# Two attention and two mixture-of-experts layers on one core: unread products, keys, row stores and a table moved

## The chip, the core and the metric

One core of a Trainium2 chip runs the whole program. The core has a matrix engine (TensorE, PE in the rows), a vector engine (VectorE, DVE), a scalar engine (ScalarE, ACT), a general one (GpSimd, POOL) and a queue engine (SyncE, SP) that computes nothing and issues DMAs; ScalarE and GpSimd issue DMAs too. Each engine works through its own list of instructions in order, and they meet at semaphores: an instruction waits until a counter has reached a value. The metric is the time of the whole program on the device, in microseconds (us), median of several runs; less is better.

## What is computed

The input x holds 32 sequences of 64 tokens with 128 values, 2048 tokens in all; ctx has the same shape.

```python
x = x + xattn0(layernorm(x), ctx, ctx)      # 16 heads of 8, biases, softmax over the 64 keys
x = x + ffn0(layernorm(x))                  # 8 experts, 2 per token, silu(x Wg) * (x Wu), inner size 176
x = x + xattn1(layernorm(x), ctx, ctx)      # as the first, other weights
x = x + ffn1(x)                             # 8 experts, 2 per token, gelu(x W1 + b1) W2 + b2, inner size 512

def ffn1(x):
    logits = xf @ gate_w                    # the router
    topk_vals, topk_idx = top_k(logits, 2)
    topk_w = softmax(topk_vals)
    ...                                     # each chosen expert's output, weighed and summed
```

## The kernel before

**Stages.** The 2048 tokens are 16 tiles of 128 and 4 groups of 512. The stages follow each other: loads and projections of the context and the queries (0 to 31 us), the first attention, the first experts (dense: every expert on every token), the second attention, and the second experts, which are sparse. Products are made of float16 pairs (a high and a low half), which is why most things exist twice.

**Keys.** The projected keys lie in k_T. SyncE copies them to `keys`, in which the four heads of a block stand in separate columns, by DMAs of 8 rows each (`place_keys`, line 343): part 0 is the first group (tiles 0 to 3), part 1 the other three, 16 DMAs each. Scores of tile 4 and later wait for the 16 DMAs of part 1. Ahead of part 1 SyncE issues the three loads of the first experts' weights (lines 368, 369; `w_g`, `w_u`, `w_d` in the trace), five loads of constants (line 371: iota8, expert_rows, table, before16, filler_rows) and the first two chunks of the second experts' weights (line 374). Behind it come seventeen stores of filler rows to sorted_rows, which wait for the constants.

**The attention's pipeline.** `attention(l)` runs `step(t)` for t from -3 on each engine. In step t TensorE turns the probabilities of tile t+1 (line 1529), turns the maxima of tile t+2 (1579), makes the scores of tile t+3 in two halves (1681, 12 matmuls each) with the fold of tile t+2's maxima between them (1602), and weighs the values of tile t. VectorE takes the scores' maxima (`TENSOR_REDUCE`, line 1026), GpSimd splits them (758, 760), ScalarE copies and takes the exponentials. The opening is the steps -3 to 1, in which the pipeline fills.

**Unread products.** `unread_products(n, bank, c0, c1)` issues n matmuls of 512 columns whose result nothing reads. Before, they stand in the first routing, in the last steps of the second attention and ahead of the second experts, and none in the opening.

**Sorting rows.** In the second attention the tokens are sorted by expert. Tiles are taken in five parts (`SORT_PARTS`: tiles 0-3, 4-7, 8-9, 10-11, 12-15). VectorE chooses the experts of a part (`choose`) two steps behind its last tile and finds its row numbers (`locate`, which ends at line 1116) a step later. GpSimd then stores each tile's normalised rows twice, once for each of its experts, with an indirect DMA to sorted_rows: `scatter(t, c)`, line 783, numbered d = 2t + c, 32 in all. `STORED` says how many have been issued at the end of each step; the rest come behind the loop. The first 24 (tiles 0 to 11) are the early ones: SyncE loads the first five slots' tiles of 256 sorted rows (line 410) when these have landed, and the later ones when all 32 have. GpSimd also computes the reciprocal deviation of each tile (`rstd`, line 740), which VectorE's `row_shift` (966) and so ScalarE's normalisation wait for.

**Tables.** With the first parts' counts VectorE makes a table of the first five slots (`early_counts`, `early_tiles`, `early_rows`), and with all of them one of the other eighteen (`late_table`), both read by SyncE and TensorE. `shares` makes the two weights of each token.

**The second experts.** For each of the 23 slots TensorE turns the rows (1835), ScalarE and VectorE split them (`arrive`, 1349 to 1355), TensorE multiplies by W1 (`up`), ScalarE takes the gelu (633), VectorE splits the hidden values (1367, 1369), TensorE multiplies by W2 (`down`, two slots behind), and GpSimd stores the result.

## Time and profile before

| | us |
|---|---|
| timed runs, median of 3 | 430.56 |
| lowest and highest | 429.47, 435.54 |
| the profiled execution | 428.84 |
| its span in the trace | 427.0 |

| engine | busy us | share of the span |
|---|---|---|
| TensorE, matmuls | 365.1 | 85% |
| VectorE | 341.2 | 80% |
| ScalarE | 268.8 | 63% |
| GpSimd | 245.7 | 58% |

The profile is of one execution. A row of its timeline gives the start of an instruction or a merged run of them, its duration, engine, line, tiles and, in brackets, how long the engine was idle ahead of it and what ended that. A busy TensorE is not TensorE at its peak: its clock has two levels, and the column PEclk tells which was granted, 1.00 (2.4 GHz) or 0.50 (1.2 GHz); at the lower one the same matmuls take twice as long.

### The profile page before, as it was taken

What the parts mean: (1) busy time and instruction counts of PE and PEld (TensorE: products, weight loads), DVE (VectorE), ACT (ScalarE), POOL (GpSimd) and SP (SyncE); (2) the same over time, 40 slices, a digit from 0 to 9 for tenths busy, and PEclk for the clock granted to TensorE, in tenths of its full rate; (3) what the DMA queues carried; (4) which work ended last, traced back from release to release, by engine and by line L of the source; (5) the groups of instructions that cost most, each with busy time, mean ns of one, the idle gap of its engine ahead of it and who ended that gap; (6) DMA issues with size and microseconds to landing.
All of it is one profiled execution on the core that took longest, in us unless ns stands there. A gap on an engine that the chain in (4) does not pass through costs nothing.

```text
span 427.0 us, 12926 instructions
## 1 busy us (share of the span) xinstructions
PE 365.1 (85%) x4528; PEld 256.8 (60%) x4528; DVE 341.2 (80%) x978; ACT 268.8 (63%) x591; POOL 245.7 (58%) x362
## 2 busy tenths in 40 slices
PE   3977799998779999999998799898878899999900
PEld 2644566666446656666655567676634798888800
DVE  6876589998888787887876689988877899999707
ACT  3664588987457555666556788786722766767504
POOL 7860367777525558576661244456787356677630
PEclk9996899999999999999999999998996999999965
DMA  7358797000001111101002400001113223232136
GB/s 202 83 166 257 218 382 266 4 3 2 2 0 51 51 52 49 48 16 40 0 11 34 62 3 2 5 21 34 40 47 102 78 79 95 78 90 65 45 103 223
DMA packets 30837, 33.15 MB, mean 78 GB/s; under 512 B 3908, under 2 KB 22606, under 8 KB 30776
## 3 DMA queue, kind: packets, MB, share of 16 engines
q1 hardware_dynamic: 27164, 25.84, 21.2%
q0 software_dynamic: 2496, 5.18, 3.6%
q10 hardware_dynamic: 1116, 1.31, 1.0%
q8 instruction: 38, 0.62, 0.6%
q14 instruction: 23, 0.19, 0.1%
HBM read 15.22 MB, written 15.01 MB: 71 GB/s over the span
## 4 chain that ended last, share of the span: by engine, by line
PE 48%; DVE 17%; SPq 10%; issue 10%; POOL 9%; ACT 3%; DMA 2%; POOLq 0%; DVEq 0%; ACTq 0%
PE ps L1433 10%; PE ps L1435 9%; PE ps L1434 9%; SPq L353 5%; PE ps L1681 4%; PE ps L1529 3%; DVE area L1026 3%; POOL sorted_rows L783 3%; POOL area L819 2%; PE ps L1602 2%; PE ps L1815 1%; SPq L371 1%; POOL expert_sums L839 1%; PE ps L1835 1%; PE ps L1443 1%
## 5 line engine op out<-in xcount | busy, mean ns | idle before, releaser
L819 POOL TENSOR_TENSOR area<-area 128x512 f16<-128x512 f32 x44 | 51.0, 1159 | 41.8 <-ACT area L587 41.8
L839 POOL DMA_INDIRECT expert_sums<-area x46 | 49.7, 1081 | 27.1 <-ACT area L609 14.4
L1433 PE MATMUL ps<-w,area 128*128 128x128 f16 (+1 forms) x360 | 63.7, 219 | 0.3 <-POOL area L819 0.2
L1434 PE MATMUL ps<-w,area 128*128 128x128 f16 (+1 forms) x360 | 63.7, 219 | 0.0
L1435 PE MATMUL ps<-w,area 128*128 128x128 f16 (+1 forms) x360 | 63.7, 219 | 0.0
L1433 PE MATMUL ps<-area,w 128*128 128x512 f16 (+1 forms) x180 | 58.8, 327 | 3.1 <-DVE area L1349 1.4
L1434 PE MATMUL ps<-area,w 128*128 128x512 f16 (+1 forms) x180 | 58.5, 325 | 0.0
L1435 PE MATMUL ps<-area,w 128*128 128x512 f16 (+1 forms) x180 | 58.4, 325 | 0.0
L1026 DVE TENSOR_REDUCE area<-ps 128x8 f32<-128x512 f32 x64 | 41.2, 686 | 14.5 <-PE ps L1681 13.2
L583 ACT ACTIVATE area<-ps 128x512 f32<-128x512 f32 x44 | 26.1, 597 | 35.1 <-PE ps L1435 34.5
L633 ACT ACTIVATE area<-ps,b_now 128x256 f32<-128x256 f32 x92 | 36.2, 477 | 12.0 <-PE ps L1435 11.9
L1276 DVE SCALAR_TENSOR_TENSOR area<-ps,area 128x512 f32<-128x512 f32 x44 | 30.1, 683 | 14.3 <-ACT area L583 14.3
L1529 PE MATMUL ps<-ident,area 128*128 128x128 f32 x256 | 37.6, 291 | 2.5 <-ACT area L508 1.5
L1433 PEld LDWEIGHTS ps<-w,area 128*128 128x128 f16 x360 | 35.2, 98 | 6.2 <-POOL area L819 1.3
L1681 PE MATMUL ps<-keys,q_T 32*64 32x256 f16 x768 | 34.8, 283 | 4.6 <-DMA keys<-area 2.4
L1434 PEld LDWEIGHTS ps<-w,area 128*128 128x128 f16 x360 | 35.2, 98 | 4.8
L783 POOL DMA_INDIRECT sorted_rows<-w,area x32 | 31.8, 995 | 10.7 <-issue 9.9
L508 ACT ACTIVATE area<-ps 128x512 f32<-128x512 f32 x64 | 34.8, 599 | 2.3 <-PE ps L1602 1.6
L1435 PEld LDWEIGHTS ps<-w,area 128*128 128x128 f16 x360 | 35.2, 98 | 0.0
L1369 DVE TENSOR_TENSOR area<-area 128x512 f16<-128x512 f32 x46 | 32.1, 698 | 1.6
L1529 PEld LDWEIGHTS ps<-ident,area 128*128 128x128 f32 x256 | 29.4, 148 | 4.6 <-ACT area L508 3.9
L758 POOL CAST area<-area 128x16 bf16<-128x16 f32 x32 | 6.3, 198 | 44.9 <-DVE area L1026 33.9
(241 smaller groups left out, 1039.4 us busy)
## 6 DMA issues: line engine op xcount, KB each, us to landing
sorted_rows<-filler_rows SPq DMA_DIRECT2D x16, 528.0 KB, 6.3
w_stage<-in_L_ffn_W SPq DMA_DIRECT2D x8, 512.0 KB, 4.0
w<-sorted_rows SPq DMA_DIRECT2D x23, 132.0 KB
keys<-area SPq DMA_DIRECT2D x32, 48.0 KB
area<-in_ctx SPq DMA_DIRECT2D x4, 256.0 KB, 4.8
keys<-expert_sums SPq DMA_DIRECT2D x4, 256.0 KB, 5.4
keys<-expert_sums ACTq DMA_DIRECT2D x4, 256.0 KB, 6.2
out<-x_res SPq DMA_DIRECT2D x8, 128.0 KB, 1.9
```

Of the source, the lines that this page charges most:

```text
L508: nc.scalar.activation(probs[:, t % 2, h * HALF:(h + 1) * HALF], ps[:, 2 * (t % 2) + h, :], ACT.Exp, scale=float(HD) ** -0.5 / ASCALE ** 2 ...
L633: nc.scalar.activation(act_f[:, n % 4, f * ST:(f + 1) * ST], ps[:, n % 4, f * ST:(f + 1) * ST], ACT.Gelu, bias=b1_now[:, 2 * u + f, j:j + ...
L783: nc.gpsimd.indirect_dma_start(out=sorted_rows, out_offset=bass.IndirectOffsetOnAxis(ap=place[:, t, c:c + 1], axis=0), in_=rows32[:, t, :] ...
L819: nc.gpsimd.tensor_tensor(hid[:, n % 4, 1, :], gated[:, n % 4, :], hid[:, n % 4, 0, :], ALU.subtract).then_inc(q["lo"], 1)
L839: nc.gpsimd.indirect_dma_start(out=expert_sums, out_offset=bass.IndirectOffsetOnAxis(ap=to_row[:, j, h:h + 1], axis=0), in_=ys[j % OUTS][: ...
L1026: nc.vector.tensor_reduce(mx[:, v, h * hh:(h + 1) * hh], ps[:, 2 * v + h, :].rearrange("p (h k) -> p h k", k=SEQ), axis=AX.X, op=ALU.max). ...
L1369: nc.vector.tensor_tensor(hid1[:, n % 8, 1, :], act_f[:, n % 4, :], hid1[:, n % 8, 0, :], ALU.subtract).then_inc(q["lo"], 1)
L1433: pe.matmul(dst, lhs[0], rhs[0], start=start, stop=False, **kw)
L1434: pe.matmul(dst, lhs[0], rhs[1], start=False, stop=False, **kw)
L1435: return pe.matmul(dst, lhs[1], rhs[0], start=False, stop=stop, **kw)
L1529: mm = pe.matmul(ps[:, 4 + h, n * P:(n + 1) * P], probs[:, t % 2, c:c + P], ident[:, :], is_transpose=True, start=(n == 0), stop=(n == 3), ...
L1681: mm = pe.matmul(ps[64 * b:64 * b + 64, 2 * v + n // 2, HALF // 2 * odd:HALF // 2 * (odd + 1)].rearrange("p (j k) -> p j k", j=QUAD), q_T[ ...
```

## The change

Five edits, none of which changes what is computed.

```diff
-STORED = {8: 2, 9: 4, 10: 6, 11: 9, 12: 11, 13: 14, 14: 16, 15: 18, 16: 20}
+STORED = {7: 2, 8: 4, 9: 6, 10: 8, 11: 11, 12: 13, 13: 16, 14: 18, 15: 20, 16: 21}
...
@@ SyncE
             place_keys(0, 0)
             for c in range(3):
                 sp.dma_start(w_stage0[c].rearrange("p (a b) -> p a b", b=w_in[c].shape[2]), w_in[c]).then_inc(s["ch0_in"], 16)
+            place_keys(0, 1)
             for dst, name in ((iota8, "iota8"), (expert_rows, "expert_rows"), (table, "table"), (before16, "before16"), (filler_rows, "filler")):
...
             load_chunk(0)
             load_chunk(1)
 
-            place_keys(0, 1)
@@ VectorE, last_steps
                     residual(LAST + 1)
+                    statistics(LAST + 1)
                     row_shift(LAST)
                     early_tiles()
-                    statistics(LAST + 1)
                     row_shift(LAST + 1)
@@ VectorE, late_table is cut in two: its start, up to last_tiles(left), is now tiles_left()
-                late_table()
-                shares()
+                tiles_left()
                 arrive(0)
                 arrive(1)
+                late_table()
                 for j in range(MT):
...
                     if j + 2 < MT:
                         arrive(j + 2)
+                shares()
@@ TensorE, project_queries
+                if l == 0 and g >= 2:
+                    unread_products(2, 0, 0, 512)
                 pe.wait_ge(KV["xt"], n + 1)
@@ TensorE, attention, ahead of the steps
                     pe.wait_ge(s["zero"], 11)
+                    unread_products(4, 0, 0, 512)
                 pe.wait_ge(KV["q_lo"], GROUPS * (l + 1))
@@ TensorE, step(t), behind the turned probabilities
                     if l == 0 and t == -2:
                         output_bias()
+                        pe.wait_ge(KV["v_lo"], 2 * GROUPS)
+                        unread_products(6, 5, 0, 512)
+                    if l == 0 and t == 0:
+                        unread_products(3, 6, 0, 512)
@@ TensorE, step(t), behind the second half of the scores
                         scores(t + 3, (t + 3) % 2, 1).then_inc(q["s_ps"], 1)
+                    if l == 0 and t == -2:
+                        unread_products(2, 5, 0, 512)
+                    if l == 0 and t == -1:
+                        pe.wait_ge(s["bo"], 2)
+                        unread_products(2, 6, 0, 512)
@@ TensorE, last_steps
-                        unread_products((1, 9, 1)[j - LAST + 1], 5, 0, 512)
+                        unread_products((1, 4, 1)[j - LAST + 1], 5, 0, 512)
                         row_logits(j)
-                    unread_products(5, 5, 0, 512)
+                    unread_products(8, 5, 0, 512)
                     part_ranks(4)
@@ TensorE, experts1
                 first_biases(0)
-                unread_products(7, 5, 0, 512)
+                unread_products(3, 5, 0, 512)
                 turn(0)
                 turn(1)
-                unread_products(4, 6, 0, 512)
+                unread_products(3, 6, 0, 512)
```

SyncE's list around the second placement of the keys (the 16 DMAs of 8x2x1536), ahead of the filler stores, first as it was:

```order
L369 DMA w<-in_L_ffn_w_d 128x11x128
L371 DMA iota<-in_iota 128x8
L371 DMA expert_rows<-in_expert_rows 128x1408
L371 DMA table<-in_table 128x192
L371 DMA before<-in_before 128x128
L371 DMA filler_rows<-in_filler 128x528
L374 DMA w_stage<-in_L_ffn_W 128x2x512 x2
L353 DMA keys<-area 8x2x1536 x16
L384 DMA sorted_rows<-filler_rows 256x1x528 x16
```

And the same place in the changed kernel:

```order
L369 DMA w<-in_L_ffn_w_d 128x11x128
L353 DMA keys<-area 8x2x1536 x16
L372 DMA iota<-in_iota 128x8
L372 DMA expert_rows<-in_expert_rows 128x1408
L372 DMA table<-in_table 128x192
L372 DMA before<-in_before 128x128
L372 DMA filler_rows<-in_filler 128x528
L375 DMA w_stage<-in_L_ffn_W 128x2x512 x2
L384 DMA sorted_rows<-filler_rows 256x1x528 x16
```

Seven loads that stood ahead of the keys stand behind them; the three weight loads stay ahead.

TensorE's list in the first attention's steps -2 and -1 (transpose of the maxima, scores and fold, turned probabilities), before the change:

```order
L1579 MATMUL ps<-identb,area 128x128
L1681 MATMUL ps<-keys,q_T 64x256 x12
L1602 MATMUL ps<-minus_ones,area 128x512 x2
L1681 MATMUL ps<-keys,q_T 64x256 x12
L1529 MATMUL ps<-ident,area 128x128 x8
```

And with it; line 1447 is the unread product:

```order
L1447 MATMUL ps<-ctx_T,wT 128x512 x6
L1590 MATMUL ps<-identb,area 128x128
L1697 MATMUL ps<-keys,q_T 64x256 x12
L1613 MATMUL ps<-minus_ones,area 128x512 x2
L1697 MATMUL ps<-keys,q_T 64x256 x12
L1447 MATMUL ps<-ctx_T,wT 128x512 x2
L1536 MATMUL ps<-ident,area 128x128 x8
```

Six products stand ahead of the first transpose and two between the scores and the turned probabilities.

VectorE's list at the start of the second experts: 1151 and 1153 end the part of the table that is now `tiles_left`, 1159 to 1178 are its second part, 1349 to 1355 an arrival of slots. Before:

```order
L1153 TENSOR_REDUCE area<-area 128x8
L1159 TENSOR_TENSOR expert_rows<-table,area 128x144
L1161 TENSOR_REDUCE area<-expert_rows 128x18
L1163 TENSOR_SCALAR area<-area 128x18
L1168 TENSOR_TENSOR expert_rows<-expert_rows,area 128x144
L1170 TENSOR_REDUCE area<-expert_rows 128x18
L1172 SCALAR_TENSOR_TENSOR area<-area,table 128x18
L1174 SCALAR_TENSOR_TENSOR area<-area 128x18
L1176 TENSOR_SCALAR area<-area 128x18
L1178 TENSOR_SCALAR area<-area,table 128x18
L1130 TENSOR_SCALAR area<-area 128x16
```

And the same place now, where 1352 to 1358 are the arrivals:

```order
L1153 TENSOR_REDUCE area<-area 128x8
L1352 TENSOR_TENSOR area<-ps,area 128x256
L1354 TENSOR_SCALAR area<-w,area 128x2
L1356 TENSOR_TENSOR area<-area,w 128x2
L1358 TENSOR_TENSOR area<-area,table 128x2
L1352 TENSOR_TENSOR area<-ps,area 128x256
L1354 TENSOR_SCALAR area<-w,area 128x2
L1356 TENSOR_TENSOR area<-area,w 128x2
L1358 TENSOR_TENSOR area<-area,table 128x2
L1159 TENSOR_TENSOR expert_rows<-table,area 128x144
```

The nine instructions of the second part stand behind the two arrivals and directly ahead of the first hidden tile; the shares (1130 and two more) have gone to the end.

## Rows read from the trace of the kernel before

**Rows 1.** Page, chain that ended last: shares of the span by engine
```profile
PE 48%; DVE 17%; SPq 10%; issue 10%; POOL 9%; ACT 3%; DMA 2%; POOLq 0%; DVEq 0%; ACTq 0%
```

**Rows 2.** Chain in order of time, 0 to 60 us: start, duration, what
```profile
26.69 1.22 SPq L369
...
27.95 4.40 SPq L371
...
35.28 0.71 SPq L353
...
46.26 2.92 DMA keys<-area
```

**Rows 3.** Timeline of TensorE, 29 to 63 us: start, duration, line, tiles, idle ahead
```profile
31.57 1.13 PE L1681 MATMUL ps<-keys,q_T 32*64 32x256 f16 x24 [1.33 <-DVE q_T L941]
...
34.75 0.29 PE L1579 MATMUL ps<-identb,area 128*128 128x128 bf16 x1 [1.60 <-POOL area L760]
...
49.22 0.53 PE L1681 MATMUL ps<-keys,q_T 32*64 32x256 f16 x12 [2.37 <-DMA keys<-area]
...
54.03 0.63 PE L1681 MATMUL ps<-keys,q_T 32*64 32x256 f16 x12
...
58.09 0.53 PE L1681 MATMUL ps<-keys,q_T 32*64 32x256 f16 x12
```

**Rows 4.** Windows: length, busy time (instructions) by engine, granted clock, DMA share, GB/s
```profile
34.00:40.00 6.00, 5.18 (x48) 3.03 (x48) 2.69 (x8) 2.50 (x6) 0.84 (x4) 0.50 0.94 302
51.00:54.00 3.00, 3.00 (x36) 2.67 (x35) 2.79 (x8) 1.92 (x4) 1.72 (x3) 0.50 1.05 388
324.00:330.00 6.00, 6.00 (x20) 3.25 (x20) 4.81 (x23) 2.49 (x6) 4.76 (x5) 0.50 0.46 137
333.00:338.00 5.00, 3.59 (x45) 3.10 (x43) 4.83 (x13) 3.90 (x12) 0.77 (x1) 1.00 0.20 57
338.00:402.00 64.00, 63.33 (x812) 57.00 (x810) 60.73 (x162) 44.15 (x119) 43.03 (x40) 1.00 0.27 77
```

**Rows 5.** DMA issues, 0 to 60 us: size of each, us from issue to landing
```profile
w<-in_L_ffn_w_d SPq DMA_DIRECT2D x1, 704.0 KB, 9.3
```

**Rows 6.** Timeline of TensorE, 307 to 345 us
```profile
324.83 3.17 PE L1443 MATMUL ps<-ctx_T,wT 128*128 128x512 f16 x7
...
335.20 0.28 PE L1433 MATMUL ps<-area,w 128*128 128x256 f16 x1 [1.41 <-DVE area L1349]
```

**Rows 7.** Timeline of VectorE, 24 to 56 us: reduces of tiles 1 and 2
```profile
37.22 1.29 DVE L1026 TENSOR_REDUCE area<-ps 128x8 f32<-128x512 f32 x2 [3.17 <-PE ps L1681]
...
41.27 1.29 DVE L1026 TENSOR_REDUCE area<-ps 128x8 f32<-128x512 f32 x2 [0.20 <-PE ps L1681]
```

**Rows 8.** Timeline of VectorE, 262 to 345 us
```profile
295.50 0.22 DVE L1116 TENSOR_REDUCE area<-area 128x8 uint32<-128x64 f32 x1
...
318.12 0.16 DVE L966 SCALAR_TENSOR_TENSOR shift<-mv_now,rstd 128x1 f32<-128x1 f32 x1 [1.07 <-POOL rstd L740]
...
325.44 0.31 DVE L1159 TENSOR_TENSOR expert_rows<-table,area 128x144 f32<-128x144 f32 x1
...
327.45 0.23 DVE L1178 TENSOR_SCALAR area<-area,table 128x18 f32<-128x18 f32 x1
...
328.88 0.42 DVE L1349 TENSOR_TENSOR area<-ps,area 128x256 f16<-128x256 f32 x1 [0.62 <-ACT area L603]
...
332.35 0.43 DVE L1367 CAST area<-area 128x512 f16<-128x512 f32 x1 [1.66 <-ACT area L633]
```

**Rows 9.** Timeline of GpSimd, 262 to 350 us
```profile
295.29 1.10 POOL L783 DMA_INDIRECT sorted_rows<-w,area  x1 [0.50 <-issue]
...
316.54 0.96 POOL L783 DMA_INDIRECT sorted_rows<-w,area  x1 [0.30 <-issue]
317.52 0.57 POOL L740 TENSOR_TENSOR rstd<-mean_var,minus_half 128x1 f32<-128x1 f32 x1
```

**Rows 10.** Timeline of SyncE, 323 to 325 us: first load of sorted rows
```profile
324.64 0.40 SPq L410 DMA_DIRECT2D w<-sorted_rows  x1
```

3 lines of the change are left out of this document (2 added, 1 removed).

## Prediction, made before the changed kernel ran

> **What bounds the kernel now.** The page's chain [rows 1] gives half of the span to TensorE and 10% to SyncE's queue, an engine that computes nothing: a queue is on the path, and the chain in order of time says where. From 27.95 to 46.9 us it is SyncE issuing DMAs, ending with the second placement of the keys [rows 2]. The TensorE rows show the other end of it: the scores of tile 4 wait 2.37 us for those keys, so TensorE stood there ready at 49.22 - 2.37 = 46.85 [rows 3]. The windows then say at which clock TensorE got there: the granted clock was 0.50 (1.2 GHz) from 34 to 40 us and again from 51 to 54 us, and it is full (2.4 GHz) in the long expert stage, where TensorE is busy 63.33 of 64 us [rows 4]. So three things bound the stretches that the change touches: keys and a halved clock in the first attention's opening, GpSimd's stores and VectorE's table work between the second attention and the experts, and TensorE itself from about 338 us to the end of the products. Work saved ahead of the expert stage moves everything behind it; TensorE time lost inside that stage is lost.
>
> **Keys ahead of the constants.** Between the load of w_d and the first key issue SyncE spends 35.28 - 27.95 = 7.33 us on seven loads. The first of them takes 4.40 us, though its data is 4 KB: it is not its own size that holds it but the 2.1 MB of expert weights queued just ahead, 704 KB each, the last issued at 26.69 and landing 9.3 us later [rows 2, 5]. An undisturbed issue here takes 0.43 (bound from the other side: 0.71, a key issue), so some 3.97 us of the 4.40 is a hold-up that will now fall on the first key issue. The placement therefore starts 7.33 - 3.97 = 3.4 us sooner. The issues themselves (from 35.28 to 46.26, at 0.73 us each) and the landing of 2.92 us behind the last stay. The keys land at 46.26 + 2.92 - 3.4 = 45.8. If the hold-up did not fall on the keys at all it would be 41.8; if it lasted until the weights have landed (26.69 + 9.3 = 36.0) it would be 49.9. I take 45.8, because the hold-up ended at 32.35 whatever came behind it. The seven loads and the filler stores behind them go out later, the loads by sixteen issues or 12 us. Their readers are the routing behind this attention, the first experts and the second attention's sort; between lie more than ten steps of 4.06 us [rows 3], which cover them. Without that cover it would be up to 12 us. SyncE also waits for VectorE's low halves of the last keys; the chain goes from issue to issue at 27.95 with no wait for VectorE in it, and if it were late, each 0.1 us would count.
>
> **Unread products in the opening.** One product costs 3.17/7 = 0.45 us at half clock [rows 6], so about 0.23 at full. Two lie ahead of each of the last two query projections, where TensorE waits for ScalarE's copy anyway; four ahead of the first scores (wait 1.33, of which GpSimd's clearing of weights takes a part); six ahead of the first transpose of maxima, where it waits 1.60 [rows 3]: 6 x 0.23 = 1.4. All hidden, at full clock. The remaining 2 + 2 + 3 lie between dependent pieces; they cost 1.6 us of TensorE, in gaps that full clock opens. 
> What that is worth is set by the engine that is next in line. The reduce of tile 1 on VectorE starts at 37.22 after 3.17 us idle [rows 7]. In front of it stand the transpose, two halves of scores and the fold, 37.22 - 34.75 = 2.5 us at half clock [rows 3] and, with ScalarE's copy of 0.3 in it that doesn't shrink, about 1.5 at full: it starts about 0.95 sooner. From there VectorE has work up to the reduce of tile 2 at 41.27, ahead of which it is idle only 0.20, and that gap goes too: 1.15, say 1.2 us sooner, and that difference is carried on. TensorE comes to tile 4 at 46.85 - 1.2 = 45.65. Keys at 45.8 and chain at 45.65 meet; either alone would have been worth little. Tile 4's scores start at 45.8 instead of 49.22: **-3.4 us**. With the wait of 2.37 gone the half-clock stretch behind it goes too: the next scores came 54.03 - 49.22 = 4.81 us later, and the undisturbed step behind that is 58.09 - 54.03 = 4.06 [rows 3]: **-0.8 us**. The opening: -4.2.
>
> **Stores a step sooner, statistics ahead.** GpSimd is two stores ahead from the seventh step on and one ahead at the end of the loop. The store's two prices are the wait for its row numbers and what it delays. At the eleventh step the first store now belongs to tile 4, whose row numbers VectorE finishes at 295.50 + 0.22 = 295.72 [rows 8]; the store stood at 295.29 [rows 9] and moves to about 296.2. That is 0.9 us on GpSimd with the deviations of tile 10 and the maxima of tile 15 queued behind it. The deviation is read at the end of VectorE's step and the maxima only behind TensorE's next transpose, so most of it is covered: I book +0.3, and +0.1 for the same at the seventh step: **+0.4** (bounds 0, all covered, and 0.9 + 0.9, none).
>
> At the end the deviation of tile 15 runs at 317.52, behind two stores (the second at 316.54; 0.96 and an idle 0.30 each, 1.27 from one to the next); VectorE's shift waits 1.07 us for it [rows 8, 9]. With its statistics taken ahead of tile 14's shift and the six table instructions behind that, some 1.6 us sooner, they are no longer late, and with one store in that place the deviation runs at 317.52 - 1.27 = 316.25. Tile 15's normalisation, its logits, the choice and the row numbers all follow 1.27 us sooner. The last early store is the fourth behind this deviation and now the third: 2 x 1.27 = 2.5 us sooner. The first load of sorted rows, issued at 324.64 [rows 10], is issued at 322.1 and lands near 324.3 (2.2 us, an estimate below the keys' 2.92 of rows 2, since this load is spread over 128 partitions).
>
> **Products and table ahead of the experts.** TensorE runs seven and four products around the first two tile transposes, at half clock (324 to 330 us [rows 4]), and VectorE works through the second table meanwhile. Now three and three. The seven start at 324.83, so now at 323.55; three take 1.35 at half clock; the transposes run from about 324.9 (the load is there), and VectorE's arrivals start at 325.9 where they started at 328.88. They take 1.8, and now the table's second part stands behind them, 325.44 to 327.68 or 2.24 us: VectorE is free for the first hidden tile at 325.9 + 1.8 + 2.2 = 329.9, against 332.35 [rows 8]: -2.4. If the eight products ahead of the last ranks hold the clock at full, everything on TensorE there halves and it is 329.1: -3.25. I take the middle, **-2.8**.
>
> That move has a price, because the table now lies between the arrivals and the first hidden tile. The products of tile 0 and 1 no longer wait, but those of tile 2 need VectorE's third arrival, behind the hidden parts of tile 0. TensorE waited 1.41 us there [rows 6]. Now VectorE reaches the first hidden tile 1.8 + 2.24 = 4.06 us after its arrivals start, where it was 332.35 - 328.88 = 3.5 [rows 8], and TensorE, with one product fewer ahead of tile 0 and those at full clock if it holds, starts that tile about 0.9 sooner after the arrivals. The wait grows by 0.6 + 0.9 to 2.9 us (bounds 1.4 + 0.6 = 2.0, and 1.4 + 2.24 = 3.6). A wait of 1.41 left the clock at 1.00 (333 to 338 [rows 4]); one of 2.37 was followed by half clock over all of 51 to 54. I take 3.4 us of it (those three and the parts around them that stretch TensorE's step to 4.81), in a stage where TensorE has 1% to spare: half of that is lost, **+1.7**.
>
> The shares, three small instructions, go into VectorE's wait for the sums at the end, which lasts through the last products, stores and loads: nothing.
>
> **The sum.** -3.4 - 0.8 + 0.4 - 2.8 + 1.7 = -4.9. The profiled execution took 428.84 us (span 427.0 and 1.8 around it): 423.9. The three timed runs have a median of 430.56, 1.7 above the profiled one; -4.9 from there is 425.7. I predict 425.0, between the two, which is -4.9 from 429.9; the rivals are counted from there.
>
> **Rivals.** (A) The clock holds through the 2.9 us wait: -6.6, 423.3. For it: 1.41 did no harm. Against: 2.37 did. Chance 0.17. The Trainium skill (TensorE: Matmul & The Clock Gate, section Why this matters for your kernels) advises against idle gaps of over about 3 us; by it a gap of 2.9 would just pass and this rival would be the result. The trace disagrees at 2.37.
> (B) The products don't keep the clock. Then the four behind the scores cost 0.45 each and the three others a part: TensorE comes to tile 4 at about 48.9, the keys are long there, and the opening gives 0.3 + 0.8 = 1.1 instead of 4.2: -1.8, 428.1. For it: GpSimd's clearing and VectorE's queries leave gaps that can't be filled. Chance 0.12.
> (C) The expert stage gives back more than the late part gained: the half clock lasts twice as long, as it did for all of 324 to 330 [rows 4], and costs 3.4 instead of 1.7: -3.2, 426.7. For it: a wait of 2.9 is longer than any other in these rows. Against: TensorE is busy without a gap behind it. Chance 0.16.
> (D) Slower. SyncE is held until the weights have landed, at 36.0, later than the 35.28 at which the placement starts now. Keys at 49.9, 0.7 later; TensorE, early by 1.2, waits 4.3 us and pays two half-clock stretches, 3.4 instead of the 0.8 of now: +0.7 + 2.6 - 0.7 (the rest of the sum) = +2.6, 432.5. It decides against the change once the keys land later than the 49.2 of now and the wait for them has grown enough to cost a second stretch; up to 49.2 the rest of the sum keeps the sign. Against it: the hold-up in the trace ends at 32.35. Chance 0.05.
>
> **Chances and range.** The forecast has 0.50. Around it 421.5 to 429.5 holds A, B, C and a microsecond of scatter either way; D and larger upsides are outside. Two per cent, 8.6 us, is about what a measurement of this kernel can tell from no change; only A with keys and chain both at their better bounds comes near it: faster 0.08, same 0.90, slower 0.02.
>
> **What would show it.** Keys: the first key issue starts at 27.95 and takes some 4.7, the last packet lands at 45 to 46; tile 4's scores wait under 0.5. Clock: 1.00 in 34 to 47; if 0.50, B. Steps behind it 4.06 apart. Deviation of tile 15 directly behind one store; first load of sorted rows 2.5 us sooner than the rest of the shift. TensorE's wait before tile 2's products: 2.9, and the clock 0.50 within 4 us of it. Wrong would be the prediction if the two halves of the opening don't meet, or if the stores' waits at steps seven and eleven are passed on in full.

## The result, and the profile after

The changed kernel takes 426.14 us (median of 20 executions, 424.07 to 431.17) beside 429.44 for the kernel before (20 executions, 427.27 to 435.54; its first three, known at the time of the prediction, had 430.56). The ratio is 0.9935, with a 95% interval of 0.9907 to 0.9963: between 1.6 and 4.0 us saved, 2.8 by the ratio, where 4.9 were forecast. (Executions over 1.5% above the fastest of their kernel are left out of the ratios but not of the medians, so the two do not divide exactly.) The profiled execution of the changed kernel, 430.2 us with a span of 428.4, is one of its longer ones, and longer than that of the kernel before (427.0). What made it longer is the main finding below.

The opening went as forecast. The timeline of TensorE of the changed kernel, 29 to 56 us (start, duration, line, tiles, idle ahead):

```profile
31.91 1.14 PE L1697 MATMUL ps<-keys,q_T 32*64 32x256 f16 x24
33.44 1.47 PE L1447 MATMUL ps<-ctx_T,wT 128*128 128x512 f16 x6
35.10 0.23 PE L1590 MATMUL ps<-identb,area 128*128 128x128 bf16 x1 [0.20 <-POOL area L760]
...
45.99 0.53 PE L1697 MATMUL ps<-keys,q_T 32*64 32x256 f16 x12
...
49.98 0.30 PE L1697 MATMUL ps<-keys,q_T 32*64 32x256 f16 x3
```

L1697 is the scores, L1447 the unread products. Where [rows 3] have waits of 1.33 and 1.60 us there are none and 0.20; the scores of tile 4 start at 45.99 with no wait for the keys (before: 49.22, after a wait of 2.37), those of tile 5 at 49.98 (54.03), those of tile 6 at 54.05 (58.09). Behind the first scores (31.91, before 31.57) tile 4 stands 14.08 us, where it stood 17.65. SyncE's share of the chain fell from the 10% of [rows 1] to 1%:

```profile
PE 51%; DVE 15%; POOL 13%; issue 11%; DMA 4%; ACT 3%; SPq 1%; POOLq 0%; ACTq 0%; DVEq 0%
```

SyncE's timeline has the sixteen key issues in one row; the kernel before first, then the changed one, in which they stand ahead of the constants:

```profile
35.28 11.66 SPq L353 DMA_DIRECT2D keys<-area  x16
```

```profile
28.04 12.94 SPq L353 DMA_DIRECT2D keys<-area  x16
```

The windows of the changed kernel (length, busy time and instructions of PE, PEld, DVE, ACT and POOL, granted clock, DMA share, GB/s):

```profile
34.00:40.00 6.00, 5.25 (x70) 2.73 (x68) 3.61 (x9) 3.15 (x7) 0.83 (x4) 1.00 0.52 89
236.00:246.00 10.00, 10.00 (x100) 6.47 (x101) 4.55 (x9) 6.18 (x13) 2.25 (x7) 0.51 0.21 30
274.00:284.00 10.00, 10.00 (x106) 7.90 (x104) 6.26 (x22) 5.37 (x13) 4.67 (x9) 0.50 0.04 14
305.00:311.00 6.00, 6.00 (x72) 4.90 (x71) 3.48 (x16) 3.75 (x9) 3.94 (x5) 0.50 0.13 41
328.00:332.00 4.00, 3.51 (x14) 1.99 (x15) 2.35 (x13) 1.15 (x5) 3.08 (x4) 0.57 0.47 154
333.00:338.00 5.00, 3.49 (x37) 3.01 (x35) 4.76 (x15) 3.89 (x12) 3.00 (x3) 1.00 0.19 61
```

The opening (34 to 40) is at full clock, where [rows 4] had 0.50. But three rows of the second attention, in which the change moves only GpSimd's stores, stand at half clock (1.2 GHz). Before, all three stretches were at 1.00 (305 to 311 too); here are the first two:

```profile
236.00:246.00 10.00, 7.69 (x138) 4.75 (x133) 6.19 (x11) 8.57 (x17) 2.37 (x7) 1.00 0.40 58
274.00:284.00 10.00, 10.00 (x174) 7.49 (x173) 9.22 (x32) 8.79 (x23) 3.82 (x8) 1.00 0.03 9
```

So the profiled execution was four microseconds ahead at 230 us and four behind at 318 us. The second attention's first scores and the residual of tile 15, before (L1681 and the first L992 row) and after (L1697 and the second):

```profile
234.29 1.14 PE L1681 MATMUL ps<-keys,q_T 32*64 32x256 f16 x24 [0.78 <-DVE q_T L941]
...
314.26 0.28 DVE L992 SCALAR_TENSOR_TENSOR x_res<-ps,x_res 128x128 f32<-128x128 f32 x1
```

```profile
230.19 1.14 PE L1697 MATMUL ps<-keys,q_T 32*64 32x256 f16 x24 [0.77 <-DVE q_T L941]
...
318.25 0.28 DVE L992 SCALAR_TENSOR_TENSOR x_res<-ps,x_res 128x128 f32<-128x128 f32 x1
```

From one to the other the kernel before needed 79.97 us and the changed one 88.06. That is where the traced gain went. The 20 times of the changed kernel differ with their mean clocks, which do not say where in the program the clock was at half: eleven lie between 424.07 and 426.32 at a mean clock of 0.959 to 0.972, one at 426.93 and 0.960, eight between 427.61 and 431.17 at 0.939 to 0.955.

The late part, VectorE's timeline (the shift and the first hidden tile) and TensorE's wait ahead of slot tile 2, in the changed kernel:

```profile
320.85 0.16 DVE L966 SCALAR_TENSOR_TENSOR shift<-mv_now,rstd 128x1 f32<-128x1 f32 x1 [0.22 <-POOL rstd L740]
...
329.50 0.42 DVE L1352 TENSOR_TENSOR area<-ps,area 128x256 f16<-128x256 f32 x1 [1.44 <-ACT area L603]
...
333.24 0.23 DVE L1178 TENSOR_SCALAR area<-area,table 128x18 f32<-128x18 f32 x1
333.38 0.42 DVE L1370 CAST area<-area 128x512 f16<-128x512 f32 x1
```

```profile
336.06 0.28 PE L1437 MATMUL ps<-area,w 128*128 128x256 f16 x1 [1.51 <-DVE area L1352]
```

The first hidden tile stands 15.13 us behind the residual of tile 15 (333.38 - 318.25), where it stood 18.09 behind it (332.35 in [rows 8], less 314.26). The shift's wait of 1.07 is 0.22. The wait ahead of slot tile 2 is 1.51, not the forecast 2.9, and 333 to 338 is at full clock. The half clock that there is stands ahead of it, at 328 to 332.

### The profile page after: what moved, and what is told of

It is laid out like the page before. It is cut to its first block, busy times and chain, and to the rows that moved or that the text cites. A ratio compares the mean times of both kernels' runs of the same rounds, so it can differ in the third digit from the quotient of the medians.

```text
span 428.4 us, 12955 instructions
## 1 busy us (share of the span) xinstructions
PE 372.4 (87%) x4542; PEld 261.3 (61%) x4542; DVE 341.1 (80%) x978; ACT 269.7 (63%) x591; POOL 242.1 (57%) x362
## 3 DMA queue, kind: packets, MB, share of 16 engines
HBM read 15.22 MB, written 15.01 MB: 71 GB/s over the span
## 4 chain that ended last, share of the span: by engine, by line
PE 51%; DVE 15%; POOL 13%; issue 11%; DMA 4%; ACT 3%; SPq 1%; POOLq 0%; ACTq 0%; DVEq 0%
PE ps L1437 9%; PE ps L1439 8%; PE ps L1438 8%; PE ps L1697 6%; POOL sorted_rows L783 5%; PE ps L1536 4%; DVE area L1026 4%; POOL expert_sums L839 3%; PE ps L1489 2%; PE ps L1509 2%; PE ps L1613 2%; POOL area L819 2%; DMA keys<-expert_sums 2%; PE ps L1831 1%; PE ps L1547 1%
## 5 line engine op out<-in xcount | busy, mean ns | idle before, releaser
L839 POOL DMA_INDIRECT expert_sums<-area x46 | 46.3, 1007 | 29.0 <-ACT area L609 18.7
L1536 PE MATMUL ps<-ident,area 128*128 128x128 f32 x256 | 39.5, 302 | 1.3 <-ACT area L508 1.0
L1697 PE MATMUL ps<-keys,q_T 32*64 32x256 f16 x768 | 35.7, 289 | 0.9 <-DVE q_T L941 0.8
L1536 PEld LDWEIGHTS ps<-ident,area 128*128 128x128 f32 x256 | 31.3, 155 | 3.3 <-ACT area L508 2.4
L758 POOL CAST area<-area 128x16 bf16<-128x16 f32 x32 | 6.3, 198 | 45.8 <-DVE area L1026 34.8
```

Of the source, the lines that this page charges most:

```text
L839: nc.gpsimd.indirect_dma_start(out=expert_sums, out_offset=bass.IndirectOffsetOnAxis(ap=to_row[:, j, h:h + 1], axis=0), in_=ys[j % OUTS][: ...
L1536: mm = pe.matmul(ps[:, 4 + h, n * P:(n + 1) * P], probs[:, t % 2, c:c + P], ident[:, :], is_transpose=True, start=(n == 0), stop=(n == 3), ...
L1697: mm = pe.matmul(ps[64 * b:64 * b + 64, 2 * v + n // 2, HALF // 2 * odd:HALF // 2 * (odd + 1)].rearrange("p (j k) -> p j k", j=QUAD), q_T[ ...
```

## Experiments

Since the clock moves everything behind it, the runs are read in four pieces that do not mix: from the first scores of attention one to those of attention two (opening and what follows), from there to tile 15's residual (second attention), from there to the first hidden tile, and from the residual to the end of the span. All runs in one table, us; "half" is the sum of the stretches at half clock inside the piece, to about a microsecond:

| kernel | median | ratio to before, 95% | to attention two | half | second attention | half | residual to hidden | residual to end |
|---|---|---|---|---|---|---|---|---|
| before | 429.44 | | 202.72 | 10 | 79.97 | 3 | 18.09 | 112.74 |
| changed | 426.14 | 0.9935 (0.9907 to 0.9963) | 198.28 | 0 | 88.06 | 27 | 15.13 | 110.15 |
| e1_keys | 429.04 | 0.9987 (0.9957 to 1.0017) | 201.19 | 14 | 82.63 | 10 | 16.73 | 111.63 |
| e2_products | 428.97 | 0.9977 (0.9950 to 1.0004) | 200.80 | 3 | 80.82 | 3 | 16.88 | 111.73 |
| e3_opening | 427.44 | 0.9940 (0.9905 to 0.9975) | 198.31 | 0 | 80.77 | 3 | 18.12 | 112.65 |
| e4_late | 428.89 | 0.9978 (0.9951 to 1.0005) | 201.10 | 14 | 80.64 | 3 | 15.12 | 110.27 |
| e5_stores | 428.37 | 0.9978 (0.9948 to 1.0007) | 198.29 | 0 | 83.50 | 14 | 18.62 | 113.25 |
| e6_fill | 426.25 | 0.9926 (0.9900 to 0.9953) | 198.31 | 0 | 85.20 | 10 | 15.22 | 110.65 |
| e7_table | 427.62 | 0.9934 (0.9893 to 0.9975) | 198.29 | 0 | 87.74 | 27 | 14.75 | 109.99 |
| e8_seven | 429.33 | 0.9947 (0.9899 to 0.9995) | 198.29 | 0 | 88.10 | 27 | 15.71 | 110.18 |
| e9_open2 | 425.39 | 0.9909 (0.9883 to 0.9935) | 198.29 | 0 | 83.79 | 14 | 15.43 | 111.31 |
| e10_all_gaps | 423.25 | 0.9859 (0.9833 to 0.9885) | 198.31 | 0 | 79.73 | 0 | 15.83 | 110.62 |
| e11_changed | 428.82 | 0.9962 (0.9929 to 0.9994) | 198.28 | 0 | 87.67 | 27 | 15.12 | 109.93 |
| e12_before_filled | 427.84 | 0.9955 (0.9925 to 0.9984) | 201.21 | 14 | 79.43 | 0 | 18.06 | 112.77 |

The medians of the kernel before, run beside each group, were 430.18 (e1 to e4), 429.23 (e5 to e8), 430.19 (e9 to e11) and 429.74 (e12). Pieces come from one traced execution each. Groups ran at different times, so kernels of different groups are compared by their ratios.

### The opening: each half alone, and both

e1 moves the keys alone:

```
             for c in range(3):
                 sp.dma_start(w_stage0[c]...).then_inc(s["ch0_in"], 16)
+            place_keys(0, 1)
             for dst, name in ((iota8, "iota8"), ...
...
-            place_keys(0, 1)
             sp.wait_ge(s["init"], 16 * 5)
```

> The kernel before with one edit: the second placement of the keys is issued ahead of the five small loads and the first chunk. My account of the opening: the keys land near 45.8 us (they did at 49.18), TensorE's chain is untouched and comes to tile 4 at 46.85, the clock is still 0.50 in 34 to 40 us. Tile 4's scores start at 46.85 with no wait (49.22 after 2.37 before), the half clock behind that wait goes, tile 6's scores start at 54.9 instead of 58.09: -3.2 us in the whole, 0.9925 of the kernel before. Rival, that the two edits of the opening have to come together: the keys alone bring under 1 us (tile 6 at 57 or later). Rival, that the first key issue is held until the weights have landed: keys at 49.9, tile 4 no sooner than before, +0.5.

e2 adds the products alone:

```
+                if l == 0 and g >= 2:
+                    unread_products(2, 0, 0, 512)
...
+                    unread_products(4, 0, 0, 512)
                 pe.wait_ge(KV["q_lo"], GROUPS * (l + 1))
...
+                        pe.wait_ge(KV["v_lo"], 2 * GROUPS)
+                        unread_products(6, 5, 0, 512)
+                    if l == 0 and t == 0:
+                        unread_products(3, 6, 0, 512)
...
+                    if l == 0 and t == -2:
+                        unread_products(2, 5, 0, 512)
+                    if l == 0 and t == -1:
+                        pe.wait_ge(s["bo"], 2)
+                        unread_products(2, 6, 0, 512)
```

> The kernel before with one edit: the unread products in the first attention's opening; the keys stay where they were. My account: the clock is 1.00 in 34 to 47 us, TensorE comes to tile 4 about 1.2 us sooner (45.65) and waits 3.6 us instead of 2.37 for keys that land at 49.2 as before; tile 4's scores start at 49.2; the longer wait is followed by half clock as the shorter one was. In the whole 0 to +0.5 us. Rival, that the products do not hold the clock: 0.50 remains in 34 to 40 us, TensorE arrives at 48.9 and waits 0.3; again no more than 0.8 saved. Rival, that a shorter stretch of half clock is worth its length anyway: -1.2.

e3 is both, and nothing of the rest.

> The kernel before with both edits of the opening and nothing else. My account: tile 4's scores at 45.8 to 46.0 with a wait under 0.5, tile 6's at 54.0, -4.2 us against the kernel before, one microsecond more than the keys alone. The late part is as before: the first hidden tile is computed as long behind tile 15's residual as before (18.1 us). Rival (the later edits carry the gain, the second attention gives the opening's gain back): under 2 us.

TensorE's timeline of e1: the keys are issued by 41.5 and are there, and still tile 4's scores (the last row) start at 48.96.

```profile
35.63 0.23 PE L1579 MATMUL ps<-identb,area 128*128 128x128 bf16 x1 [1.60 <-POOL area L760]
...
41.86 2.12 PE L1529 MATMUL ps<-ident,area 128*128 128x128 f32 x8
...
48.96 0.86 PE L1681 MATMUL ps<-keys,q_T 32*64 32x256 f16 x12
```

Its windows show why: the clock did not come back at 41 us, as it had in the trace of the kernel before.

```profile
34.00:40.00 6.00, 4.33 (x45) 2.75 (x48) 3.23 (x7) 2.12 (x5) 0.83 (x4) 0.70 0.51 89
40.00:49.00 9.00, 9.00 (x98) 5.50 (x92) 5.87 (x14) 5.72 (x12) 2.73 (x6) 0.50 0.68 181
```

e4 and e12 have the opening of the kernel before unchanged, and their executions did the same: half clock for 14 us in one piece, 201.1 and 201.2 us to the second attention. Tile 4's scores in e4's timeline have no wait for the keys, though the keys come as late as before:

```profile
49.12 0.53 PE L1685 MATMUL ps<-keys,q_T 32*64 32x256 f16 x12
```

Against those, e1's 201.19 is no gain at all. My -3.2 for the keys alone was wrong (by the times -0.6, between -1.8 and +0.7): it took the 46.85 of one execution for the time at which TensorE arrives, and that hung on when the clock came back. Why it comes back at 41 us in one execution and at 49 in others is not shown. In e2's trace TensorE is as expected: TensorE arrives 14.14 us behind its first scores (33.05; 15.28 before, so 1.14 sooner, forecast 1.2), waits for the keys, and half clock follows the wait (49 to 53). The scores of tile 4 in its timeline:

```profile
48.79 0.53 PE L1693 MATMUL ps<-keys,q_T 32*64 32x256 f16 x12 [1.60 <-DMA keys<-area]
```

To the second attention e2 needs 200.80, 0.3 less than e4. By the times it gains 1.0 us (-2.1 to +0.2), which does not tell my 0 to +0.5 from the rival's -1.2.

Together, e3 needs 198.31 us, 2.8 less than e4 and e12 and 4.4 less than the trace of the kernel before. All nine traces with the complete opening give 198.28 to 198.31, at full clock. The two edits do have to meet; measured, the pair is worth 2.6 us by the ratio of e3 (1.1 to 4.1), where I expected 4.2. The products both close gaps and add to TensorE's busy time, and no run tells which of the two holds the clock.

### The late edits alone, the stores, the table, the seven products

e4 is the changed kernel with the edits of e1 and e2 taken out again.

> The changed kernel with the two edits of the opening undone, so only the stores a step sooner, the statistics of tile 15 ahead, the split table and the moved products remain. The opening is as before (tile 4's scores at 49.22). From tile 15's residual to the first hidden tile 15.1 us, where the kernel before has 18.1 and the changed one 15.1; wait ahead of slot tile 2's products 1.4 to 1.6 with the clock at 1.00. In the whole -2.4 to -2.8 us (0.994). If opening and late part add up, the changed kernel should be 6.6 us faster than before; it was measured 3.3 faster, so a rival is that something between them costs 3 us: then this kernel alone shows under 1 us of gain.

The piece from the residual to the first hidden tile is 15.12, the same as in the changed kernel and 3.0 below 18.1. To the end of the span the gain is 2.5 against the kernel before. But e1 and e2, which have none of the late edits, end at 111.6 and 111.7; ahead of the experts their clock was at half for 3 us, and for 7 in before, e3 and e12, which end at 112.7 to 112.8. e4 has 3 as well, and against e1 and e2 the late edits are worth 1.4. The median says 0.9 us (ratio, -2.1 to +0.2), below what I expected. The rival's number, under 1 us, came true, but not its reason that something between costs 3, since the second attention took 80.64. Opening and late part, 2.6 and 0.9 by their ratios, make 3.5, and the changed kernel 2.8: they add up within the intervals.

e5 puts the stores back:

```
-STORED = {7: 2, 8: 4, 9: 6, 10: 8, 11: 11, 12: 13, 13: 16, 14: 18, 15: 20, 16: 21}
+STORED = {8: 2, 9: 4, 10: 6, 11: 9, 12: 11, 13: 14, 14: 16, 15: 18, 16: 20}
```

> The changed kernel with one part undone: the stores are placed one step later again, as in the kernel before. Theory (the stores cost what I booked): GpSimd's waits of 0.64 and 0.74 us at the eleventh step and of 1.88 at the seventh go, about 0.4 us sooner at the residual of tile 15; the last early store and the first load of sorted rows come 1.27 us later and the deviation of tile 15 is back behind two stores, with the table's first part to hide it. From the residual of tile 15 to the end 111.4 us (112.74 before, 110.15 in the changed kernel). In the whole +0.5 to +1.0 us against the changed kernel. Rival (the waits at the stores hand their delay on to TensorE and are what costs the second attention its time): from the second attention's first scores to the residual of tile 15 it takes 2 us less than in the changed kernel in the median, and this kernel is the faster one by 1 us or more.

GpSimd's timeline of e5, and below it VectorE's shift of tile 15:

```profile
315.08 1.03 POOL L783 DMA_INDIRECT sorted_rows<-w,area  x1 [0.20 <-issue]
316.42 0.96 POOL L783 DMA_INDIRECT sorted_rows<-w,area  x1 [0.30 <-issue]
317.40 0.57 POOL L740 TENSOR_TENSOR rstd<-mean_var,minus_half 128x1 f32<-128x1 f32 x1
```

```profile
318.00 0.16 DVE L966 SCALAR_TENSOR_TENSOR shift<-mv_now,rstd 128x1 f32<-128x1 f32 x1 [1.47 <-POOL rstd L740]
```

The deviation of tile 15 starts 3.25 us behind its residual (314.15), as in the kernel before (317.52 - 314.26 = 3.26), though the statistics are ahead here. In the changed kernel it is 2.00 (320.25 - 318.25). So the statistics' new place alone brings nothing while two stores stand in front. The stores alone would not have brought the 1.26 us either. In VectorE's timeline of the kernel before the last of tile 15's statistics is

```profile
316.90 0.15 DVE L962 TENSOR_SCALAR mean_var<-mv_now 128x1 f32<-128x1 f32 x1
```

and ends at 317.05, 2.79 behind the residual, where the deviation started at 3.26: with one store fewer and the statistics late it could have started some 0.5 sooner (an estimate from this row; no run has the stores alone). This is a second pair that has to meet. The first load of sorted rows is 10.34 behind the residual (324.49), before 10.38, changed 7.84 (326.09): the 2.5 us hang on the stores, and by the same estimate in part on the statistics. The end cannot be compared, since e5's trace has half clock over nearly all of 318 to 333:

```profile
318.00:333.00 15.00, 14.10 (x65) 8.77 (x66) 9.50 (x57) 4.86 (x13) 9.64 (x10) 0.54 0.31 90
```

On the price of the earlier stores: from the wait at step eleven to the residual, e5 takes 22.05 us and e3, with the stores late too, 22.06; e4, with them early, 22.2. From the first scores to that wait e4 takes 58.4, e2 and e3 58.7 to 58.8, so nothing is lost there. The stores' waits cost at most 0.1 to 0.2 us, not the 2 that the rival wanted and less than the 0.4 I booked. GpSimd's wait for row numbers is there (0.64 us at 297.99 in the changed kernel), but it is covered.

e7 computes the second table in one piece again, e8 puts seven and four products back:

```
                 tiles_left()
+                late_table()
                 arrive(0)
                 arrive(1)
-                late_table()
```

```
-                unread_products(3, 5, 0, 512)
+                unread_products(7, 5, 0, 512)
                 turn(0)
                 turn(1)
-                unread_products(3, 6, 0, 512)
+                unread_products(4, 6, 0, 512)
```

> The changed kernel with the second table's experts and rows computed in one piece, ahead of the arrivals, as before. In the trace of the changed kernel VectorE is idle 1.44 us ahead of the arrivals and the table's second part takes 2.14 behind them; in one piece the arrivals start 0.8 later and the first hidden tile is no longer held by the table but by ScalarE. Theory: the split is worth next to nothing, the first hidden tile stands 15.1 +-0.4 us behind tile 15's residual as with the split. Rival (the split is what brought the hidden tile forward): 17 or more, +2 us in the whole.

> The changed kernel with seven and four unread products around the first two tile transposes ahead of the experts, instead of three and three. Theory: the loads of the sorted rows land while the seven run, so the transposes start some 1.1 us later (4 x 0.27, as the three took 0.82 in the trace of the changed kernel), the first hidden tile by 1.1 to 1.4 us, from tile 15's residual to the end 111.3. Rival (the extra products hold the clock at full where it fell at 328, and pay for themselves): 0 to -0.5 us.

With the table in one piece the first hidden tile is 14.75 us behind the residual and the end 109.99; with it split 15.13 and 110.15. The split is worth nothing or less. With seven and four products the hidden tile is 0.58 later and the end the same (110.18): less than the 1.1 to 1.4 I expected, and nothing by the end. So what is left of the late part is mainly the stores with the statistics; the moved products of the last steps and the shares were not tried alone.

### Where the second attention's clock goes

e11 is the changed kernel once more.

> The changed kernel once more, beside the two with filled gaps: 426.1 median, as before. If the place of the half clock differs from execution to execution, its trace shows a second attention of other length than the 88.06 us of the first trace, 80.8 at the shortest.

The median was 428.82 and not the 426.1 expected, 2.7 us above the median of the first 20 executions of the same kernel. Its trace has 87.67 us in the second attention, with falls at 235, 276 and 303. Of the twelve times five are 425.81 to 427.59 at a clock of 0.951 to 0.960, seven 428.00 to 430.37 at 0.939 to 0.950. So what varies with the time is how long the clock is at half; the ratio this time was 0.9962, and 0.9935 the first time, within each other's intervals. In the timeline of TensorE of e11, these gaps stand ahead of the falls, the first three within 7 us; behind the one at 294 the clock did not fall here, but in the kernel before it fell behind the same gap (293 to 296):

```profile
230.20 1.14 PE L1697 MATMUL ps<-keys,q_T 32*64 32x256 f16 x24 [0.77 <-DVE q_T L941]
233.38 0.23 PE L1590 MATMUL ps<-identb,area 128*128 128x128 bf16 x1 [0.58 <-POOL area L760]
235.88 1.97 PE L1536 MATMUL ps<-ident,area 128*128 128x128 f32 x8 [1.04 <-ACT area L508]
274.71 0.33 PE L1718 MATMUL ps<-ident,w 128*128 128x128 f32 x1 [1.68 <-DVE area L978]
294.02 0.33 PE L1718 MATMUL ps<-ident,w 128*128 128x128 f32 x1 [1.38 <-DVE area L978]
303.84 0.27 PE L1590 MATMUL ps<-identb,area 128*128 128x128 bf16 x1 [1.79 <-issue]
```

The test is to fill them. e6 was the first try:

```
+                else:
+                    unread_products(3, 0, 0, 512)
                 pe.wait_ge(KV["q_lo"], GROUPS * (l + 1))
...
+                    if l == 1 and t == -2:
+                        unread_products(2, 2, 0, 512)
+                    if l == 1 and t == TILES - 3:
+                        unread_products(6, 0, 0, 512)
...
+                        if l == 1:
+                            unread_products({6: 5, 10: 5, 12: 3}.get(t, 0), 2 * v, 0, 512)
                         scores(t + 3, v, 0).then_inc(q["s_half"], 1)
...
+                    if l == 1 and t == -2:
+                        unread_products(4, 6, 0, 512)
```

> The changed kernel with 28 further unread products in the second attention, at its gaps of TensorE (0.77, 0.58, 1.04 us in the opening; 1.68 and 1.38 at the steps that take in a choice; 0.9 and 1.78 at the end). Theory (those gaps are what the clock falls after, and which of them it falls after differs from execution to execution; that is where the opening's gain goes): the granted clock is 1.00 in all of 230 to 315, the second attention takes 80 us or less from its first scores to tile 15's residual (88.06 in the trace of the changed kernel, 79.97 before), the median is 424.0 or less and the spread of the times narrower by a half. Rival (the clock falls whatever the gaps are): stretches of half clock remain in 236 to 312, median 426 as the changed kernel. Rival (the products delay their own stage): clock 1.00, but no gain.

Half of it hit. The three gaps of the attention's opening are gone and so is the fall at 236; the gap at step thirteen is gone. But the products for the gaps of 1.68 and 1.39 were one step early: TensorE's timeline shows them at 264.08, where it had no wait, and the gap as large as ever behind.

```profile
264.08 1.24 PE L1447 MATMUL ps<-ctx_T,wT 128*128 128x512 f16 x5
...
271.33 0.44 PE L1728 MATMUL ps<-ident,w 128*128 128x128 f32 x1 [1.68 <-DVE area L978]
```

In that place five of them cost 1.0 of their 1.24 us: 40.18 us from the first scores to the gap, where e1 to e4 have 39.2. With ten us at half clock behind the two gaps the attention took 85.20. Median 426.25, no gain. e9 keeps the four places that hit (the first, second, third and last of the products above) and leaves out the three that missed; e10 adds to e9 products at the right steps, behind the scores, where the wait is:

```
+FILLED = {7: 10, 11: 8}
...
+                        if l == 1 and t in FILLED:
+                            pe.wait_ge(q["mt"], T + 3)
+                            pe.wait_ge(q["res"], T - 1)
+                            unread_products(FILLED[t], 7, 0, 256)
                         pe.wait_ge(q["on"], 2 * T)
```

> The changed kernel with unread products at four gaps of the second attention only: three ahead of its first scores (gap of 0.77 us), two ahead of the first transpose of maxima (0.58), four ahead of the first turn of probabilities (1.04), six ahead of the transpose of maxima at step 13 (1.78). The run with 28 products showed no fall at 236 us, but put 13 of them one step ahead of the gaps of 1.68 and 1.38, where they only delayed. Theory (falls follow gaps): clock 1.00 from 230 to 268 and from 296 to 312; the gap of 1.68 is open, so a fall after it stays in most executions. From the second attention's first scores to tile 15's residual 80.8 us (as in the trace with the opening alone, where the clock fell once, for 3.4 us), median 424.5 to 425.0. Rival (opening's gain is lost in another way): median 426 or more.

> The same with ten and eight products of half the width in the gaps of 1.68 and 1.38 us at steps seven and eleven, into columns that nothing reads, where TensorE waits for VectorE's quotients anyway. Theory (falls follow gaps): clock 1.00 over the whole of 230 to 315, second attention 79.5 us from first scores to the residual, median 423.5 to 424.3. Rival (the products there delay VectorE's or TensorE's next work by as much as they fill): clock 1.00 and second attention over 80.8. Rival (falls come without gaps): stretches of half clock remain in 236 to 312.

e10's timeline and windows:

```profile
268.23 1.26 PE L1448 MATMUL ps<-ctx_T,wT 128*128 128x256 f16 x10
269.77 0.33 PE L1731 MATMUL ps<-ident,w 128*128 128x128 f32 x1 [0.28 <-DVE area L979]
...
288.05 0.33 PE L1731 MATMUL ps<-ident,w 128*128 128x128 f32 x1 [0.33 <-DVE area L979]
```

```profile
230.00:315.00 85.00, 78.95 (x1200) 54.55 (x1199) 71.64 (x268) 61.07 (x148) 47.53 (x79) 1.00 0.12 28
```

The ten products fill 1.26 of the 1.68; the gap's end, 39.2 us behind the first scores, did not move. The clock is full over all of 230 to 315, the second attention takes 79.73 us, and the six times lie between 422.23 and 423.73 at a clock of 0.974 to 0.976: a spread of 1.5 us where the changed kernel has 7.1 in its 20 executions and 4.6 in the twelve of e11, run beside e10. 423.25 is the best of all the kernels here, 1.4% below the kernel before (1.2 to 1.7). e9, with the two gaps of 1.68 and 1.39 open, has no fall at 236 and one behind each of the two:

```profile
269.89 0.33 PE L1726 MATMUL ps<-ident,w 128*128 128x128 f32 x1 [1.68 <-DVE area L978]
290.52 0.33 PE L1726 MATMUL ps<-ident,w 128*128 128x128 f32 x1 [1.39 <-DVE area L978]
```

```profile
271.00:278.00 7.00, 7.00 (x85) 5.04 (x81) 4.44 (x16) 3.89 (x10) 3.34 (x6) 0.53 0.04 13
292.00:298.00 6.00, 6.00 (x71) 4.67 (x67) 4.29 (x15) 2.87 (x6) 2.87 (x5) 0.50 0.04 13
```

Its second attention took 83.79 us, not the 80.8 expected (two falls of 7 instead of one of 3), and its median of 425.39 is 0.4 above the range given.

e9's trace also shows, by chance, the wait that the prediction had and the changed kernel had not. TensorE's timeline, the start of slot tile 0 and the wait ahead of slot tile 2, and the window behind it:

```profile
326.62 0.28 PE L1437 MATMUL ps<-area,w 128*128 128x256 f16 x1 [0.33 <-DVE area L1352]
...
332.67 0.39 PE L1437 MATMUL ps<-area,w 128*128 128x256 f16 x1 [2.52 <-DVE area L1352]
```

```profile
332.00:336.00 4.00, 3.33 (x21) 2.52 (x22) 3.79 (x13) 1.40 (x4) 1.39 (x2) 0.57 0.10 34
```

The forecast had TensorE start slot tile 0 about 0.9 us sooner behind the arrivals, if the clock holds. In e9 it holds from 322 to 331, and tile 0 starts 0.58 us behind the first arrival (326.04); before it was 1.47 (330.35 - 328.88). In the changed kernel the clock falls at 328, ahead of it, and tile 0 starts 1.44 behind (329.50):

```profile
330.94 0.42 PE L1437 MATMUL ps<-area,w 128*128 128x256 f16 x1
```

From the first hidden tile to the end e9 takes 95.9 us and the changed kernel 95.0: the long wait, with half clock behind it, costs about 0.9 us. (e9's end, 111.31, is 1.2 longer in all; 0.3 of that lies ahead of the hidden tile.)

e12 puts the same products into the kernel before, with nothing of the change.

> The kernel before with the products of the last run in the second attention's gaps, and nothing of the change. Theory (three parts that add up once the clock holds: opening 4.1, late part 1.4, gaps 1.3 to 1.5): the kernel before already had no fall at 236 us in its trace and lost little in this attention, so here the products bring 1.3 to 1.5 us (79.7 instead of 80 to 81 from first scores to the residual of tile 15), 428.8 beside 430.2, ratio 0.997. Rival (the filled gaps alone bring most of the 6.9 us between the kernel before and the last run): 425 or less.

The second attention is at full clock and takes 79.43 us; 0.9955 of the kernel before, -1.9 us (0.7 to 3.2), slightly more than the 1.3 to 1.5 expected. The opening is as in e4 (201.21), the end as before (112.77). Between e12 and e10 lies the change and nothing else, now with the second attention's clock held in both: 427.84 and 423.25, 4.6 us by the medians, 4.1 by the two ratios (0.9955 - 0.9859, times 430; from their intervals, an estimate, 2.4 to 5.8). Without the products it showed 2.8 and 1.6. The same products are worth 1.9 us in the kernel before and 4.4 in the changed one (e10 beside e11: 0.9962 - 0.9859), so the two do not simply add.

## Why the prediction was right, and where it wasn't

The time (426.1 in 421.5 to 429.5) and the case (within 2%, a little faster) came out as given, but the sum was 2 us too good, and that it came so near is in part luck: its terms are off by more than the sum, in opposite directions. Point by point:

- **Keys ahead of the constants.** Right in direction, mis-sized, and it did not matter. The hold-up behind the weights was not 3.97 us on the first key issue: sixteen issues took 12.94 us where they had taken 11.66, so 1.3 us fell on them (1.5 in e1, whose weight issues took what they took before). The issues end at 40.98 instead of 46.94, six us sooner and not 3.4, so the keys land, with the 2.92 of [rows 2], at about 43.2 and not at 45.8. TensorE arrives at 45.99 (forecast 45.65, and both are 14.08 behind the first scores of their trace): it, not the keys, sets tile 4's start.
- **Products in the opening.** Right: clock 1.00 in 34 to 40, waits of a few tenths, TensorE 1.14 sooner in e2 against 1.2. Opening as a whole: 4.04 us at tile 6 and 4.10 at the second attention's first scores (4.4 counted from the first attention's first scores), forecast 4.2.
- **But what that is measured against** was one execution of the kernel before. e4 and e12, with the same opening code, lost 1.5 us less in it (201.1 and 201.2 against 202.72). Against those the opening is worth 2.8. The sentence that each half alone is worth little held for both; my own numbers for e1 contradicted it, and the sentence was right.
- **Second attention.** Here is the step that failed. The sum carried the opening's gain through to the end and had no term for the clock of the eighty microseconds between. The nine traces with the opening show that its piece is carried (198.3 each time), and then the second attention takes anything from 79.7 to 88.1 us, by whether the clock falls after gaps of 0.6 to 1.8 us that were there before. With them filled in both kernels the change is worth 4.1 to 4.6 us (e12 and e10), near the 4.9, but not by the terms of the sum: in the two traces 2.9 come from the opening (forecast 4.2), 2.15 from the end (forecast 2.8 - 1.7 = 1.1), and 0.3 are lost in the second attention (forecast 0.4).
- **Stores.** Booked +0.4, shown 0.1 to 0.2. The 1.27 us at tile 15's deviation is right to a few hundredths, and so is its reason: it takes the stores and the statistics together (e5, and the row of the kernel before beside it). First load of sorted rows 2.5 us sooner: shown 2.54.
- **Late part, -2.8.** 2.96 us to the first hidden tile in the changed kernel, within the bounds. The split table brought nothing of it (e7), and the products taken out ahead of the experts 0.58 us, which were gone by the end (e8). To the end, with equal half clock, the late edits are worth 1.4 (e4 beside e1 and e2), more than the 2.8 - 1.7 = 1.1 of the sum, since the +1.7 did not come.
- **Wait ahead of slot tile 2, +1.7.** Forecast 2.9 with half clock behind. It was 1.51 and 1.72 in the two traces of the changed kernel, with full clock. The time is then rival A's, but not its mechanism: the clock did not hold through a wait of 2.9, the wait did not come. What was wrong is the 0.9 us by which TensorE was to start slot tile 0 sooner: the clock fell ahead of it. Only e9 has the clock held there, and it shows 2.52 and half clock, at a price of about 0.9 instead of 1.7. So the term describes one case in several, not the rule; this error and the missing term of the second attention pull opposite ways, which is part of why the total stayed in range.
- **Rival B** (products don't hold the clock) fell with the windows; **D** (keys held till the weights land) with 12.94; **C** had a time near the one measured, 426.7, but from a stage where nothing of the kind happened.

The Trainium skill (TensorE: Matmul & The Clock Gate, section Why this matters for your kernels) asks for no idle gaps of over about 3 us. The longest gap in the second attention is 1.8 us, and by that rule it should have stayed at full clock; the traces disagree (0.50 in 274 to 284 us behind a gap of 1.68), and with the gaps of 0.6 to 1.8 us filled the clock held in the traces of e10 and e12.

What stays open: why the fall at 236 us comes with the earlier opening. Five of the six traces with that opening and the three gaps unfilled have it (changed, e5, e7, e8, e11; not e3), none of the four with the late opening and the same gaps unfilled (before, e1, e2, e4). Gaps seem to be needed, since none of e6, e9 and e10, which have them filled, has it; that gaps alone decide is not shown, nor whether it is the gap or TensorE's share of busy time that counts, which the products change together. Nor is the median worth of the stores, since e5's interval overlaps that of the changed kernel.

## What to carry to other kernels

Where the clock falls after short gaps of TensorE, a gain ahead of such a stretch has to be counted with what the stretch can lose, and a single trace of the kernel before shows only one of its outcomes: compare pieces between fixed landmarks over several traces, and look at the spread of the times with their mean clocks before forecasting from any one. Unread products earn their place only where TensorE waits for something that does not wait for them; five of them one step too early cost 1.0 of their 1.24 us. And two edits that shorten two sides of a meeting point are to be tried together before either is judged.

## What the runs showed of the hardware

- Gaps of 0.77, 0.58 and 1.04 us close together, or a single one of 1.39 or 1.68 (e9), are followed by 3 to 17 us at 1.2 GHz; in other traces in which that stretch of the program is the same, the same gaps are followed by none (the three in e1 to e4, the 1.38 in e11, the 1.69 in the kernel before).
- What a fall costs, read between the second attention's first scores and the gap at step seven: 39.2 us without one (e1 to e4), 42.0 with ten us at half clock (272.17 - 230.19 in the changed kernel), 44.5 with seventeen (274.71 - 230.20 in e11).
- Within one kernel the mean granted clock goes with the time: in the changed kernel 0.943 with 430.2 us and 0.962 with 424.8. It does not order different kernels: e2 took 428.35 us at 0.966.
- The hold-up behind 2.1 MB of weights was 3.97 us on the issue of one small load, and 1.3 us (1.5 in e1) over all sixteen key issues in the same place: the price was not that of the place in the queue.
